# First layer's attention sums: products of rows one and two apart, two rows at a time, with three products in place of four

## The chip, the cores and the metric

The kernel runs on one core of a Trainium2 chip. The metric is device time in microseconds (us) of one launch; lower is better. The engines named below are TensorE (PE, with its weight loads shown as PEld), VectorE (DVE), ScalarE (ACT), GpSimd (POOL) and SyncE (SP, which here issues DMAs).

## The reference

Four layers run one after the other on x of shape (4, 48, 256, 256) in float32, each on the group-normed x and added to it. The change lies in the first layer alone. That layer makes q, k and v by a 1x1 and a depthwise 3x3 convolution and mixes the 48 channels of v by a softmax of the normalised products q k^T over all 65536 pixels.

```python
def _gn(v, G=16, eps=1e-5):
    g = v.reshape(B_, G, C_ // G, H_, W_)
    m = jnp.mean(g, axis=(2, 3, 4), keepdims=True)
    s = jnp.var(g, axis=(2, 3, 4), keepdims=True)
    return ((g - m) / jnp.sqrt(s + eps)).reshape(v.shape)

def _L0_conv_ref(x, qkv_w, dw_w, proj_w, temperature):     # x: (4, 48, 256, 256), f32
    qkv = lax.conv_general_dilated(x, qkv_w, (1, 1), 'VALID', dimension_numbers=DN)
    qkv = lax.conv_general_dilated(qkv, dw_w, (1, 1), ((1, 1), (1, 1)), feature_group_count=3 * c, dimension_numbers=DN)
    q, k, v = jnp.split(qkv, 3, axis=1)
    ...
    q = _l2_normalize(q)
    k = _l2_normalize(k)
    attn = jax.nn.softmax(jnp.einsum('bhcn,bhdn->bhcd', q, k) * temperature, axis=-1)
    out = jnp.einsum('bhcd,bhdn->bhcn', attn, v).reshape(b, c, h, w)
    return lax.conv_general_dilated(out, proj_w, (1, 1), 'VALID', dimension_numbers=DN)
...
x = x + _L0_conv_ref(_gn(x), ...)
x = x + _L1_conv_ref(_gn(x), ...)   # recurrences over rows and columns
x = x + _L2_conv_ref(_gn(x), ...)   # 8x8 patches, products of spectra
x = x + _L3_conv_ref(_gn(x), ...)   # 8x8 patches, mask on spectra, 3x3, gelu
return x
```

## The kernel before

The first stage, `stage_l0_attention`, never builds q and k. All that the attention matrix needs of a picture are sums over pixels of x(p) x(p + shift)^T for the shifts that two 3x3 windows can have between them. With a column of ones added to the 48 channels (C1 = 49), each such sum is a 49x49 product with the pixels as the contracted dimension. The stage collects 29 of them (`l0_terms`): for rows two apart and rows one apart five column shifts each (tile `rows_` in PSUM, 10 x 49 columns), for shifts within a row three (`same`), and terms for the borders (`same` again and `edges`). Afterwards TensorE multiplies them from right and left by the folded weights (`mix_right`, `mix_left`), VectorE multiplies with the taps and adds up, and softmax follows.

**Data.** `x_px` holds the picture as 128 blocks (4 pictures x NBLK = 32) of R = 8 rows. A row is [128 partitions, 6, 49]: 128 pixel pairs, six column positions. Even and odd pixels are two products (`for odd in range(2)`), whose results go to PSUM partitions 0 to 48 and 64 to 112 (ODD = 64), that is to two halves of TensorE's columns. SyncE loads a block (1176 KB) into one of BUF = 4 slots of `l0a_x`, as soon as block n - 3 is used up (semaphore `used`, incremented by the last product of a block).

**Order on TensorE.** Everything is written out by hand. For each row y, `lines` issues one `line` into `same` (147 columns) and then two into `rows_` (245 columns each): the row with the one before it (dy = 1) and with the one two before it (dy = 2), which may lie in the slot before. A line is two matmuls, and each float32 matmul stands in the trace as two instructions. The stationary operand is 49 columns of the earlier row, the moving operand the current row. The first block of a picture is written apart (row 0 has no dy = 1, row 1 no dy = 2), so is the last pass, and the passes between are a hardware loop over four blocks. Between the rows of a picture's first blocks stand the small steps of the picture before: `group_sums` after row (0, 5), `mixing_matrix` after (1, 4), `mix_right` and `mix_left` in block 2, `turn_sum` after row 5 of block 3. In the last pass `turn_scores` and `mix_projection` follow.

**End of a picture.** `borders` puts the column borders into `edges` and increments `sums_done`. Then ScalarE copies the even halves of `same`, `rows_` and `edges` to `r` in SBUF (`r_act`), VectorE the odd halves of `same` and `rows_` (`r_dve`), and TensorE waits for both before the next picture. From `r` VectorE makes the moments of the group norm, and `group_sums` takes them. After the fourth picture the small steps run one after the other with nothing beside them. GpSimd has no work in this stage.

## Time and profile before

| | |
|---|---|
| median of 3 runs | 11938.39 us (11927.18 to 11943.02) |
| profiled execution, its own time | 11946.39 us |
| span of its trace | 11944.6 us |
| TensorE busy over the span | 11372.6 us (95%) |
| VectorE busy | 7033.3 us (59%) |
| ScalarE busy | 5102.7 us (43%) |
| GpSimd busy | 4884.2 us (41%) |
| mean granted clock of TensorE | 0.981 |

The busy times are unions: matmuls overlap each other, so the mean duration of one is longer than what it costs in a row of them. What one costs is therefore read from the distance of starts. The granted clock is a share of full speed; 1.00 is 2.4 GHz and 0.50 is 1.2 GHz.

### The profile page before, as it was taken

Reading aid. Unit: us, or ns where it says so; the run is one execution under the profiler, and the core shown is the slowest. Engines: PE = TensorE matmul, PEld = TensorE weight load, DVE = VectorE, ACT = ScalarE, POOL = GpSimd, SP = SyncE. Lnnn points to the kernel's source line nnn. Section 1 sums busy time; section 2 is a strip of 40 time slices with the busy share of each in tenths; the row PEclk is TensorE's granted clock in tenths of the full one; section 3 lists DMA queues with packets and bytes.
Section 4 is the critical chain, followed back from the end, with each engine's and each line's share of the span. In section 5 each row is a group of like instructions: output and inputs, shape, how many; then the busy total and the mean of one; then the engine's idle time right before and its main releaser. Section 6 shows DMA issues by size and latency. Waiting matters only on the chain. (4 is left out here: it accounts for less than half of the span.)

```text
span 11944.6 us, 374350 instructions
## 1 busy us (share of the span) xinstructions
PE 11372.6 (95%) x155430; PEld 7933.0 (66%) x155430; DVE 7033.3 (59%) x16042; ACT 5102.7 (43%) x10598; POOL 4884.2 (41%) x4142
## 2 busy tenths in 40 slices
PE   8999999989998999899999999999999899889988
PEld 7877544489996777555555555555555577777776
DVE  0000355544444544588888888888888666656665
ACT  0000111134343334355555555555555567767766
POOL 0000122211340025466666666666666444444444
PEclk9999999999998999899999999999999999999999
DMA  4333466597695468866666666666666333333333
GB/s 140 130 133 132 123 160 159 153 159 140 116 163 156 149 178 228 164 85 89 88 88 88 88 88 88 88 88 88 88 89 88 91 104 106 105 96 105 107 103 94
DMA packets 2387653, 1411.49 MB, mean 118 GB/s; under 512 B 1889330, under 2 KB 2260809, under 8 KB 2313245
## 3 DMA queue, kind: packets, MB, share of 16 engines
q1 hardware_dynamic: 2111384, 1290.01, 53.5%
q10 hardware_dynamic: 275072, 105.14, 3.8%
q8 instruction: 797, 13.06, 0.5%
q14 instruction: 400, 3.28, 0.1%
HBM read 646.26 MB, written 449.27 MB: 92 GB/s over the span
## 5 line engine op out<-in xcount | busy, mean ns | idle before, releaser
L1795 PE MATMUL l_m<-l_wa,l_pix 128*128 128x288 f32 x8192 | 2211.2, 413 | 2.7 <-DVE l_wb L1977 2.7
L1795 PEld LDWEIGHTS l_m<-l_wa,l_pix 128*128 128x128 f32 x8192 | 1475.3, 190 | 688.6 <-issue 361.6
L1651 POOL TENSOR_TENSOR l_qkv<-l_qkv,l_copies 128x576 f32<-128x576 f32 x1024 | 1437.1, 1403 | 631.0 <-DVE l_qkv L1988 620.2
L1641 POOL TENSOR_TENSOR l_pix<-l_raw 128x516 f32<-128x516 f32 x1024 | 1217.3, 1189 | 1042.1 <-DVE l_t L2025 1017.2
L1476 PE MATMUL l1h_ps<-l1h_ring,l1h_w 96*96 96x256 f32 x6120 | 1327.3, 379 | 61.5 <-ACT l1h_ring L1418 58.6
L1476 PEld LDWEIGHTS l1h_ps<-l1h_ring,l1h_w 96*96 96x96 f32 x6120 | 998.9, 163 | 389.7 <-issue 58.8
L1509 DVE SCALAR_TENSOR_TENSOR l1h_ring<-l1h_ps,l1h_bias,l1h_columns 96x256 f32<-96x256 f32 x1020 | 670.7, 658 | 677.3 <-PE l1h_ps L1476 671.6
L509 PE MATMUL l0a_rows<-l0a_x 128*49 128x245 f32 x8144 | 1044.2, 371 | 0.0
L870 PE MATMUL l0b_bank<-l0b_x,l0b_w 49*64 49x512 f32 x9216 | 1001.0, 593 | 4.4 <-DVE l0b_w L896 4.4
L1890 ACT ACTIVATE l_ks<-l_f 94x384 f32<-94x384 f32 x1024 | 498.0, 486 | 842.8 <-PE l_f L1810 842.8
L1810 PE MATMUL l_f<-l_qkv,l_a 64*94 64x384 f32 x4096 | 834.7, 483 | 1.6 <-POOL l_qkv L1651 1.5
L870 PEld LDWEIGHTS l0b_bank<-l0b_x,l0b_w 49*64 49x64 f32 x9216 | 437.2, 133 | 565.2 <-issue 565.2
L1801 PE MATMUL l_m<-l_wb,l_left 58*128 58x288 f32 x4096 | 774.2, 455 | 0.0
L1460 POOL TENSOR_TENSOR l1h_columns<-l1h_blocks,l1h_ring 96x2048 f32<-96x2048 f32 x63 | 350.8, 5589 | 1033.1 <-DVE l1h_ring L1509 1033.1
L1901 ACT ACTIVATE l_y<-l_i,l_shift,l_rsd 128x96 f32<-128x96 f32 x2048 | 709.3, 427 | 14.4 <-DVE l_shift L2015 0.6
L1895 ACT ACTIVATE l_sd<-l_mv,l_eps 128x4 f32<-128x4 f32 x512 | 152.2, 297 | 1288.3 <-DVE l_mv L2008 1288.3
L1224 PE MATMUL l1v_ps<-l1v_ring_w,l1v_w 48*48 48x130 f32 x20480 | 632.7, 272 | 46.7 <-ACT l1v_ring_w L1147 41.4
L509 PEld LDWEIGHTS l0a_rows<-l0a_x 128*49 128x49 f32 x8144 | 601.9, 124 | 108.4 <-issue 2.8
L1224 PE MATMUL l1v_ps<-l1v_ring_p,l1v_w 48*48 48x128 f32 x20320 | 616.0, 269 | 7.5 <-issue 7.2
L1224 PEld LDWEIGHTS l1v_ps<-l1v_ring_w,l1v_w 48*48 48x48 f32 x20480 | 586.8, 120 | 50.0 <-issue 50.0
L2568 DVE TENSOR_TENSOR l_gate<-l_turn 128x768 f32<-128x768 f32 x384 | 428.0, 1129 | 301.7 <-ACT l_turn L2478 301.7
L1985 DVE TENSOR_TENSOR l_qkv<-l_m,l_copies 128x288 f32<-128x288 f32 x1024 | 461.9, 451 | 238.4 <-ACT l_copies L1881 223.6
(275 smaller groups left out, 21684.5 us busy)
## 6 DMA issues: line engine op xcount, KB each, us to landing
l0a_x<-x_px_dram SPq DMA_DIRECT2D x128, 1176.0 KB, 5.2
l_edge<-l_turn SPq DMA_DIRECT2D x384, 236.2 KB
l0b_x<-x_in_dram SPq DMA_DIRECT2D x128, 493.8 KB
l_raw<-l_raw SPq DMA_DIRECT2D x128, 483.6 KB, 7.3
l_raw<-x_dram SPq DMA_DIRECT2D x1270, 48.0 KB, 3.7
l_out<-x_dram SPq DMA_DIRECT2D x264, 192.0 KB, 3.6
x_dram<-l0b_out ACTq DMA_DIRECT2D x256, 193.5 KB, 3.1
out_dram<-l_out SPq DMA_DIRECT2D x516, 96.0 KB, 2.0
```

The source lines that it names most:

```text
L509: last = nc.tensor.matmul(o[odd * ODD:odd * ODD + C1, lo:lo + n * C1], x[:, ks, ys, 2 + odd, :], x[:, k, y, e0 + odd:e0 + odd + n, :].rear ...
L870: last = nc.tensor.matmul(bank[2 * n + rt][h * HI:(h + 1) * HI, :], w[part, t, :], rows(part, k, 4 * n + h + t // 3 - rt)[:, :, t % 3:t % ...
L1224: last = nc.tensor.matmul(ps[g][side(c), r, 0:width], w[side(r), t, :], x, start=(t == 0), stop=(t == TAPS - 1), skip_group_check=True)
L1476: last = nc.tensor.matmul(ps[g][0:C2, 0:GI * V], w[:, kernel, s, :], ring[:, g, before % DEEP, :, s:s + V], start=(s == 0), stop=(s == 2))
L1509: nc.vector.scalar_tensor_tensor(out=ring[:, g, x % DEEP, :, 1:V + 1], in0=ps[g][0:C2, 0:GI * V].rearrange("p (i v) -> p i v", i=GI), scal ...
L1641: nc.gpsimd.tensor_tensor(pix[:, n % 2, i, half * HALF:(half + 1) * HALF].rearrange("p (r w) -> p r w", w=PW), in0, in1, op).then_inc(pix_ ...
L1651: nc.gpsimd.tensor_tensor(q, q, copies[:, g % 2, 1:2, :].broadcast_to([128, 2, OUTC]), ALU.add)\
L1795: last = nc.tensor.matmul(bank[i][:, 0:OUTC], pix[:, k, i, first:first + 128], wa[:, b, i, :], start=True, stop=(i in (1, 2)))
L1801: nc.tensor.matmul(bank[i][:, 0:OUTC], left[rows, k, first:first + 128], wb[rows, b, :], start=False, stop=True).then_inc(conv_done, 1)
L1810: last = nc.tensor.matmul(f[0:SLOTS, h, 0:2 * QK].rearrange("p (n o) -> p n o", n=2), a[k, 0:SLOTS], qkv[k, j % 4, 2 * r:2 * r + 2, 0:QK], ...
L1890: nc.scalar.activation(ks[:, r % 2], f[0:SLOTS, :, 0:2 * QK].rearrange("p h (n o) -> p h n o", n=2)[:, :, :, C2:QK], ACT.Copy).then_inc(k_ ...
L1901: last = nc.scalar.activation(y[:, g, m, :], iv[:, m * C2:(m + 1) * C2], ACT.Identity, scale=rsd[:, g, m:m + 1], bias=shift[:, g, m:m + 1])
```

## The change

Rows are taken in pairs. Call the two rows of a pair e (even) and h (odd), the pair before them z and m. Before, rows one apart need <e,h> + <m,e>, and rows two apart <m,h> + <z,e>, where <a,b> is the product of a line with a as stationary and b as moving operand. After, three products are made:

- <m, e + h> into a new PSUM tile `mids`,
- <e - m, h> into the first half of `rows_`,
- <z - m, e> into its second half.

`rows_` first half + `mids` is <e,h> + <m,e>, second half + `mids` is <m,h> + <z,e>. GpSimd makes e + h (`both`, 294 elements per partition) and the two differences (`less`, 98 each) for every pair, one `tensor_tensor` each, and counts them on `paired`, on which TensorE waits once for each pair. Two blocks of `both` and `less` exist (SLOTS = 2): GpSimd starts on block n when n is loaded and block n - 2 is used up. At the end of a picture VectorE adds `mids` to both halves of `r`, in four additions of 49 x 245, before it signals `r_dve`. `edges` now shares the PSUM bank of `zb[0]`. The first pair of a picture has only <e,h>, as before.

```diff
--- before.py
+++ after.py
@@ -423,6 +423,7 @@
     CHUNKS = -(-TERMS // CHUNK)
     EDGE, CORNER = 13, 25
     NCH = 25
+    PAIRS, SLOTS, FORMS = R // 2, 2, 3
     with nc.cleanup_on_exit(), ExitStack() as ctx:
         def sb(name, shape):
             return ctx.enter_context(nc.sbuf_tensor(f"l0a_{name}", shape, F32))
@@ -433,6 +434,8 @@
         def sem(name):
             return nc.alloc_semaphore(f"l0a_{name}")
         x = sb("x", [128, BUF, R, 6, C1])
+        both = sb("both", [128, SLOTS, PAIRS, 6, C1])
+        less = sb("less", [128, SLOTS, PAIRS, 2, 2, C1])
         xc, xk = sb("xc", [128, B, 2, 2, 3, C1]), sb("xk", [4, B, 5, C1])
         first, others = sb("first", [9, O]), sb("others", [9, TERMS, O])
         wt, h = sb("wt", [O, TERMS, O]), sb("h", [O, TERMS, O])
@@ -448,8 +451,9 @@
         n2, rn = sb("n2", [O, 1]), sb("rn", [O, 1])
         sc, e, at = sb("sc", [C, C]), sb("e", [C, C]), sb("at", [C, O])
         mx, sm, rs = sb("mx", [C, 1]), sb("sm", [C, 1]), sb("rs", [C, 1])
-        rows_, same, edges = pb("rows"), pb("same"), pb("edges")
+        rows_, same, mids = pb("rows"), pb("same"), pb("mids")
         zb, qb, small = [pb("z0"), pb("z1")], [pb("q0"), pb("q1")], pb("small")
+        edges = zb[0]
         consts, cleared, w_done, w_out, w_ready = (sem(n) for n in ("consts", "cleared", "w_done", "w_out", "w_ready"))
         taps_in = sem("taps_in")
         loaded = [sem(f"loaded{k}") for k in range(BUF)]
@@ -457,6 +461,8 @@
         chain, spread, rooted, a_done = (sem(n) for n in ("chain", "spread", "rooted", "a_done"))
         z_done, z_out, q_done, h_out = (sem(n) for n in ("z_done", "z_out", "q_done", "h_out"))
         p_turned, turned, exped, mixed = (sem(n) for n in ("p_turned", "turned", "exped", "mixed"))
+        paired, copied = sem("paired"), sem("copied")
+        flat = x[:].rearrange("p k r e c -> p (k r) e c")
         block = ctx.enter_context(nc.Block())
 
         def terms(c):
@@ -501,33 +507,52 @@
             pe.wait_ge(cleared, 2)
             pe.wait_ge(consts, 16 * 9)
 
-            def line(k, y, dy, o, lo, begin, end):
-
-                ks, ys = ((k * R + y - dy) // R) % BUF, (y - dy) % R
-                e0, n = (2, 3) if dy == 0 else (0, 5)
+            def line(k, y, lo, begin, end):
+
                 for odd in range(2):
-                    last = nc.tensor.matmul(o[odd * ODD:odd * ODD + C1, lo:lo + n * C1], x[:, ks, ys, 2 + odd, :],
-                                            x[:, k, y, e0 + odd:e0 + odd + n, :].rearrange("p e c -> p (e c)"),
+                    last = nc.tensor.matmul(same[odd * ODD:odd * ODD + C1, lo:lo + 3 * C1], x[:, k, y, 2 + odd, :],
+                                            x[:, k, y, 2 + odd:5 + odd, :].rearrange("p e c -> p (e c)"),
                                             start=begin, stop=end, skip_group_check=True)
                 return last
+
+            def cross(o, lo, left, right, begin, end):
+
+                for odd in range(2):
+                    last = nc.tensor.matmul(o[odd * ODD:odd * ODD + C1, lo:lo + 5 * C1], left[:, odd, :],
+                                            right[:, odd:odd + 5, :].rearrange("p e c -> p (e c)"),
+                                            start=begin, stop=end, skip_group_check=True)
+                return last
+
+            def pair(turn_of_k, k, y, top, end):
+
+                here, above = k * R + y, (k * R + y - 2) % (BUF * R)
+                if top and y == 1:
+                    return cross(rows_, 0, flat[:, here - 1, 2:4], flat[:, here], True, end)
+                i = y // 2
+                begin = top and y == 3
+                pe.wait_ge(paired, turn_of_k * (BUF * PAIRS * FORMS) + (k * PAIRS + i + 1) * FORMS)
+                cross(mids, 0, flat[:, above, 2:4], both[:, k % SLOTS, i], begin, end)
+                cross(rows_, 0, less[:, k % SLOTS, i, 0], flat[:, here], False, end)
+                return cross(rows_, 5 * C1, less[:, k % SLOTS, i, 1], flat[:, here - 1], begin, end)
 
             def lines(turn_of_k, k, y, top, bottom):
 
                 if y == 0:
                     pe.wait_ge(loaded[k], turn_of_k * 16 + 16)
                 row = y if top else R
-                last = line(k, y, 0, same, 0, row == 0, bottom and y == R - 1)
-                for dy in (1, 2):
-                    if row >= dy:
-                        last = line(k, y, dy, rows_, (dy - 1) * 5 * C1, row == dy, bottom and y == R - 1)
+                line(k, y, 0, row == 0, bottom and y == R - 1)
                 if row == 0:
-                    line(k, y, 0, same, 3 * C1, True, True)
+                    line(k, y, 3 * C1, True, True)
                 if bottom and y == R - 1:
-                    line(k, y, 0, same, 6 * C1, True, True)
+                    line(k, y, 6 * C1, True, True)
+                if y % 2 == 1:
+                    last = pair(turn_of_k, k, y, top, bottom and y == R - 1)
                 if y == R - 1:
                     last.then_inc(used, 1)
 
             def borders(b):
+                if b > 0:
+                    pe.wait_ge(z_out, b * CHUNKS)
                 for col in range(2):
                     for half in range(2):
                         nc.tensor.matmul(edges[0:C1, col * 3 * C1:(col + 1) * 3 * C1], xc[:, b, half, col, 0, :],
@@ -664,8 +689,14 @@
                     dve.wait_ge(z_done, b * CHUNKS)
                 nc.vector.tensor_copy(r[ODD:LAST, 10:19, :].rearrange("p t c -> p (t c)"), same[ODD:LAST, 0:9 * C1])
                 nc.vector.tensor_copy(r[ODD:LAST, 0:10, :].rearrange("p t c -> p (t c)"), rows_[ODD:LAST, 0:10 * C1])\
-                    .then_inc(r_dve, 1)
+                    .then_inc(copied, 1)
+                dve.wait_ge(copied, b + 1)
                 dve.wait_ge(r_act, b + 1)
+                for lanes in (slice(0, C1), slice(ODD, LAST)):
+                    for dy in range(2):
+                        part = r[lanes, 5 * dy:5 * dy + 5, :].rearrange("p t c -> p (t c)")
+                        last = nc.vector.tensor_tensor(part, mids[lanes, 0:5 * C1], part, ALU.add)
+                last.then_inc(r_dve, 1)
                 dve.wait_ge(r_dve, b + 1)
                 nc.vector.tensor_copy(mom[:, 0:1], r[:, 10, C:C1])
                 nc.vector.tensor_tensor_reduce(out=junk[0:LAST, :], in0=r[:, 10, :], in1=diag[0:LAST, :], scale=1.0, scalar=0.0,
@@ -733,6 +764,32 @@
                 dve.wait_ge(mixed, b + 1)
                 nc.vector.tensor_copy(S["mt"][:, b * C:(b + 1) * C], small[0:C, 384:384 + C]).then_inc(chain, 1)
 
+        @block.gpsimd
+        def _(pool):
+
+            def pairs(i, k, first):
+
+                pool.wait_ge(loaded[k], i * 16 + 16)
+                for n in range(PAIRS):
+                    here = k * R + 2 * n + 1
+                    a, m, z = here - 1, (here - 2) % (BUF * R), (here - 3) % (BUF * R)
+                    if first and n == 0:
+                        pool.sem_inc(paired, FORMS)
+                        continue
+                    nc.gpsimd.tensor_tensor(both[:, k % SLOTS, n], flat[:, a], flat[:, here], ALU.add).then_inc(paired, 1)
+                    nc.gpsimd.tensor_tensor(less[:, k % SLOTS, n, 0], flat[:, a, 2:4], flat[:, m, 2:4], ALU.subtract)\
+                        .then_inc(paired, 1)
+                    nc.gpsimd.tensor_tensor(less[:, k % SLOTS, n, 1], flat[:, z, 2:4], flat[:, m, 2:4], ALU.subtract)\
+                        .then_inc(paired, 1)
+            for k in range(BUF):
+                if k >= SLOTS:
+                    pool.wait_ge(used, k - 1)
+                pairs(0, k, k == 0)
+            with pool.Fori(1, B * PASSES) as i:
+                for k in range(BUF):
+                    pool.wait_ge(used, i * BUF + (k - 1))
+                    pairs(i, k, False)
+
 
 def norm_weights(nc, dve, S, b, e, tmp, lb, lb_ready, chain, after):
```

TensorE in the hardware loop, before: the first three rows of a block, where each line in `same` is followed by its two lines in `rows_`.

```order
L509 MATMUL l0a_same<-l0a_x 49x147 [waits l3w_done0]
L509 MATMUL l0a_same<-l0a_x 49x147
L509 MATMUL l0a_rows<-l0a_x 49x245 x4
L509 MATMUL l0a_same<-l0a_x 49x147 x2
L509 MATMUL l0a_rows<-l0a_x 49x245 x4
L509 MATMUL l0a_same<-l0a_x 49x147 x2
L509 MATMUL l0a_rows<-l0a_x 49x245 x4
```

The same place after, two pairs of rows (semaphore l3w_done0 is the number that `loaded1` has here, REGISTER_ALU computes the count to wait for):

```order
L513 MATMUL l0a_same<-l0a_x 49x147 [waits l3w_done0]
L513 MATMUL l0a_same<-l0a_x 49x147 x3
L533 REGISTER_ALU
L521 MATMUL l0a_mids<-l0a_both,l0a_x 49x245 [waits l0a_paired]
L521 MATMUL l0a_mids<-l0a_both,l0a_x 49x245
L521 MATMUL l0a_rows<-l0a_x,l0a_less 49x245 x4
L513 MATMUL l0a_same<-l0a_x 49x147 x4
L533 REGISTER_ALU
L521 MATMUL l0a_mids<-l0a_both,l0a_x 49x245 [waits l0a_paired]
L521 MATMUL l0a_mids<-l0a_both,l0a_x 49x245
L521 MATMUL l0a_rows<-l0a_x,l0a_less 49x245 x4
```

A pair of rows has 4 matmuls of 147 columns in a row and then 6 of 245, where it had 4 and 8 in turns of 2 and 4.

VectorE at the end of the first picture, before:

```order
L665 COPY l0a_r<-l0a_same 49x441 [waits l3w_consts,l0a_sums_done,l3w_cleared,l3w_scaled]
L666 COPY l0a_r<-l0a_rows 49x490
L670 COPY l0a_mom<-l0a_r 113x1 [waits l0a_r_dve,l0a_r_act]
L671 ISA l0a_junk,l0a_mom<-l0a_r,l0a_diag 113x49
```

And after:

```order
L690 COPY l0a_r<-l0a_same 49x441 [waits l3w_consts,l0a_sums_done,l3w_cleared,l3w_scaled]
L691 COPY l0a_r<-l0a_rows 49x490
L698 TENSOR_TENSOR l0a_r<-l0a_mids,l0a_r 49x245 [waits l0a_r_act,l0a_copied]
L698 TENSOR_TENSOR l0a_r<-l0a_mids,l0a_r 49x245 x3
L701 COPY l0a_mom<-l0a_r 113x1 [waits l0a_r_dve]
L702 ISA l0a_junk,l0a_mom<-l0a_r,l0a_diag 113x49
```

Four additions stand between the copies and the moments; TensorE's next picture waits for `r_dve` behind them.

## Rows read from the trace of the kernel before

**Rows 1.** Instructions of line L509: duration ns min/median/max, first and last start.

```profile
L509 PEld LDWEIGHTS l0a_rows<-l0a_x x8144: 122/124/208, 138.1 to 1294.8; 128*49 128x49 f32 x199
L509 PE MATMUL l0a_rows<-l0a_x x8144: 367/370/615, 138.3 to 1295.0; 128*49 128x245 f32 x199
L509 PE MATMUL l0a_same<-l0a_x x4128: 286/288/482, 136.8 to 1295.4; 128*49 128x147 f32 x197
```

**Rows 2.** Busy times by window; the first line names the columns.

```profile
core 0: us, PE busy (x) PEld busy (x) DVE busy (x) ACT busy (x) POOL busy (x), PEclk, DMA share, GB/s
...
300.00:400.00 100.00, 100.00 (x1118) 84.49 (x1116) 0.00 (x0) 0.00 (x0) 0.00 (x0) 1.00 0.38 136
...
136.00:140.00 4.00, 3.15 (x22) 2.70 (x24) 0.00 (x0) 0.00 (x0) 0.00 (x0) 0.50 1.05 435
140.00:144.00 4.00, 4.00 (x32) 2.81 (x30) 0.00 (x0) 0.00 (x0) 0.00 (x0) 0.66 1.03 446
```

**Rows 3.** Timeline inside a picture: start us, duration us, engine, line, instructions.

```profile
603.07 1.03 PE L509 MATMUL l0a_rows<-l0a_x 128*49 128x245 f32 x8
603.69 0.37 PEld L509 LDWEIGHTS l0a_same<-l0a_x 128*49 128x49 f32 x4
603.89 0.46 PE L509 MATMUL l0a_same<-l0a_x 128*49 128x147 f32 x4
...
604.15 1.03 PE L509 MATMUL l0a_rows<-l0a_x 128*49 128x245 f32 x8
604.27 0.33 SPq L479 DMA_DIRECT2D l0a_x<-x_px_dram  x1
...
605.22 1.03 PE L509 MATMUL l0a_rows<-l0a_x 128*49 128x245 f32 x8
```

**Rows 4.** Timeline at the end of the first picture.

```profile
417.37 0.57 ACT L630 ACTIVATE l0a_r<-l0a_edges 49x490 f32<-49x490 f32 x1
...
418.00 0.96 PE L509 MATMUL l0a_same<-l0a_x 128*49 128x147 f32 x12 [1.62 <-ACT l0a_r L630]
...
418.79 0.62 PE L509 MATMUL l0a_rows<-l0a_x 128*49 128x245 f32 x4
...
419.67 1.86 PE L509 MATMUL l0a_rows<-l0a_x 128*49 128x245 f32 x8
...
421.80 1.41 PE L509 MATMUL l0a_rows<-l0a_x 128*49 128x245 f32 x8
...
423.03 0.42 PE L509 MATMUL l0a_same<-l0a_x 128*49 128x147 f32 x4
```

**Rows 5.** Groups by line and shape on VectorE: busy us, mean ns of one.

```profile
L697 DVE TENSOR_TENSOR l0a_h<-l0a_q,l0a_wt 96x480 f32<-96x480 f32 x20 | 13.1, 654 | 65.2 <-PE l0a_q L564 65.2
...
L706 DVE TENSOR_TENSOR l0a_pp<-l0a_s 96x96 f32<-96x96 f32 x4 | 1.0, 254 | 0.1
```

**Rows 6.** Timeline before `turn_sum` of the first picture.

```profile
457.04 0.46 PE L509 MATMUL l0a_same<-l0a_x 128*49 128x147 f32 x4
...
462.15 0.82 DVE L704 TENSOR_REDUCE l0a_s<-l0a_h 96x96 f32<-96x384 f32 x1
...
463.64 0.29 PE L569 MATMUL l0a_small<-k_ident,l0a_pp 96*96 96x96 f32 x1
```

**Rows 7.** Additions of two SBUF tiles on GpSimd: duration ns min/median/max.

```profile
L1651 POOL TENSOR_TENSOR l_qkv<-l_qkv,l_copies x1024: 1389/1403/1417, 5035.5 to 9404.1; 128x576 f32<-128x576 f32 x171
...
L2637 POOL TENSOR_TENSOR l_turn<-l_turn,l_edge x192: 2202/2235/3026, 9468.7 to 11903.1; 128x960 f32<-128x960 f32 x192
...
L1460 POOL TENSOR_TENSOR l1h_columns<-l1h_blocks,l1h_ring x63: 5519/5587/5627, 4325.9 to 4968.2; 96x2048 f32<-96x2048 f32 x63
```

**Rows 8.** GpSimd's timeline, two additions one behind the other.

```profile
7001.00 1.09 POOL L1641 TENSOR_TENSOR l_pix<-l_raw 128x516 f32<-128x516 f32 x1 [2.39 <-DVE l_t L2025]
7002.06 1.41 POOL L1651 TENSOR_TENSOR l_qkv<-l_qkv,l_copies 128x576 f32<-128x576 f32 x1
```

**Rows 9.** The loads of `l0a_x`, from issue to landing.

```profile
DMA to landing us min/median/max: 4.9/5.2/13.0
```

## The prediction

> **What bounds the kernel now.** I read three views, from coarse to fine. The first, the instructions of line L509 [rows 1], gives the length of the stage that changes: its products run from 136.8 to 1295.4 us, 1158.6 us of a span of 11944.6. Nothing outside it is touched, and a stage starts only when the one before it has ended, so what this stage loses or gains goes into the end one to one. The second, busy time by window [rows 2], shows who sets the pace: from 300 to 400 us TensorE is busy 100.00 of 100 us at granted clock 1.00 (2.4 GHz), VectorE, ScalarE and GpSimd 0.00, the DMA share is 0.38. So TensorE bounds the stage, and GpSimd is empty. The third, the timeline within a picture [rows 3], gives the price of one instruction by distances of starts. The 8 instructions into `rows_` take 603.07 to 603.89 = 0.82 us, 102.5 ns each; the 4 into `same` take 603.89 to 604.15 = 0.26 us, 65 ns each. A row is 1.08 us, a block of 8 rows about 8.62 us (5.38 us for five rows of the same timeline would give 8.61). The duration of one (370 and 288 ns in the middle [rows 1]) is no price: they overlap.
>
> 245 columns cost 102.5 ns and 147 cost 65, 0.42 and 0.44 ns per column. The price follows the columns that stream, not the number of instructions.
>
> **The term that the change is made for.** A pair of rows has 8 instructions into `same` and 16 into `rows_` before, 8 and 12 of 245 columns after. Before it is 2.15 us, after 8 x 0.065 + 12 x 0.1025 = 0.52 + 1.23 = 1.75 us. Removed: 4 x 0.1025 = 0.41 us. There are 512 pairs (4 pictures x 128), of which the 4 first ones of a picture stay as they are. 508 x 0.41 = **208.3 us off**. Block time falls to 7.0 us.
>
> Does the new order (8 instructions of `same` in a row instead of 4) keep the price? At a picture's start 12 of them stand in a row [rows 4]: 418.00 to 418.79 is 0.79 us, 66 ns each. Yes.
>
> **GpSimd's side, the unknown.** Each pair needs one addition of 294 elements and two of 98. No GpSimd addition that small is in the trace. From [rows 7], the fastest of 960 (2202 ns) and of 576 (1389 ns) give a slope of 813/384 = 2.12 ns per element and 170 ns fixed. 490 x 2.12 + 3 x 170 = 1.55 us per pair, 6.2 us per block, against TensorE's 1.75 and 7.0. The next one starts a little before the last has ended [rows 8] (1.06 us after one of 1.09), so this is rather high. Other ends: at the pace of the 96 x 2048 additions, (5587 - 170)/2048 = 2.65 ns, a pair is 1.81 us, 0.06 over TensorE's; at the slowest of the 960 ones, (3026 - 170)/960 = 2.98 ns, it is 1.97 us, 0.22 over. I take 1.55: both slow rows are from stages where VectorE works beside GpSimd, and here it is idle. GpSimd may run up to a block ahead, since it starts on block n when TensorE leaves n - 2, so at 1.55 the sums are ready some 5 us before their pair, and the work costs nothing. If that cover went, each 0.1 us per pair would cost 51 us.
>
> **Loads.** GpSimd needs block n one block earlier than TensorE. The load is issued when block n - 3 is used up, lands in 5.2 us [rows 9], and GpSimd wants it 7.0 us later: 1.8 us to spare. The longest, 13.0 us, would be 6 us late; GpSimd's lead of 5 us hides most of that. The DMA share of 0.38 [rows 2] becomes 0.38 x 8.62/7.0 = 0.47. Nothing is added.
>
> **TensorE's 508 added waits.** A wait that is already fulfilled stands in the trace at each block's start, on `loaded`. One lies at about 604.1 us, just ahead of the SyncE issue at 604.27 that the end of the block releases; the rows start 1.08 us before it and 1.07 us after it [rows 3]. Price nil, and I take that, the same kind of wait before the same kind of matmul. Upper end: the start of L569 comes about 0.1 us later than its row's 0.82 us lead to (462.71 + 0.82 for the last row, against 463.64 [rows 6]), though it is another shape as well. 508 x 0.1 would be 51 us.
>
> **End of a picture.** VectorE adds four times 49 x 245 behind its copies. From [rows 5], 654 ns for 480 elements and 254 for 96: 1.04 ns per element, so 254 + 149 x 1.04 = 409 ns each, 1.6 us for four. Before, both waits of TensorE ended with ScalarE's L630 at 417.94 and the next picture began at 418.00 [rows 4]. ScalarE still ends there, and the additions wait for it, so the whole 1.6 us is on the path. It hits three times between pictures and once at the end, where `group_sums` waits for the moments: 4 x 1.6 = **6.4 us lost**. Queued behind the wait is the whole next picture.
>
> **The step `turn_sum`.** It waits for VectorE's sums, which end at 462.15 + 0.82 = 462.97, plus 0.25 for `pp`: 463.22 [rows 5, 6]. Before, six rows stood ahead of it, 457.04 + 6.5 = 463.5, so it came just too late to wait. After, three pairs take 3 x 1.75 = 5.25 us: TensorE is there at 462.3 and waits 0.9 us. Three pictures: **2.8 us lost**. This is the one small step whose cover goes; the others have several us.
>
> **The clock.** After the stop of 1.62 us at 418.00, TensorE ran at full pace, then from 419.67 to about 423 at half pace (1.2 GHz): 2.13 us for a row instead of 1.08 and 1.23 us for 8 instructions instead of 0.82, 1.46 us lost [rows 4]. After the longer emptiness before the stage it ran at 0.50 and then 0.66 [rows 2]: 3.15 x 0.5 + 4 x 0.34 = 2.9 us lost. The stop now becomes 3.2 us, so the loss is between these, 0 to 1.5 us more each. I take half: 3 x 0.75 = **2.2 us**.
>
> **Sum.** 208.3 - 6.4 - 2.8 - 2.2 = 196.9 us less. The profiled execution, 11946.4 us, would be 11749.5. It lies 8.0 us above the median of the runs (11938.4), so the median after is 11741.5 us. The forecast's own range, from its clock and load terms, is 11725 to 11765; with the upper end of the waits 11793.
>
> **Rivals.**
>
> 1. GpSimd sets the pace. For it: at 89% of TensorE's pace it has little room, its price is extrapolated, and both slow rows lie above 1.75. Against it: VectorE is idle beside it. Price: 508 x 0.06 = 30 us at the pace of the 2048 ones (11772), 508 x 0.22 = 112 us at the slowest of the 960 ones (11853).
>
> 2. Weight loads set the pace in the long run of `same`. Loads of four take 0.37 us [rows 3] against 0.26 of streaming. If they paced it, 8 would cost 0.74 instead of 0.52: 508 x 0.22 = 112 us, also 11853. Against it stand the 12 at 66 ns [rows 4]. A sharper form is that no load hides. Then a removed instruction would also give back its load of 124 ns [rows 1], 508 x 4 x 0.124 = 252 us, and the time would be 11490. But 12 loads of 124 ns stand in each row of 1.08 us, less than their sum of 1.49, so they do overlap. The Trainium skill (TensorE: Matmul & The Clock Gate, The mechanism) says that a weight load overlaps with running matmuls only where the row groups differ; all of these use 128 rows, and by that rule 11490 would be the time. The trace does not agree.
>
> 3. **Slower than before:** TensorE catches up with GpSimd, stops, and falls to 1.2 GHz again and again. One such fall costs 1.46 us [rows 4]. With GpSimd at 1.97 us per pair, a block is 7.87 us, and with one fall 9.33 instead of 8.62: 127 x 0.71 = 90 us more than before, 12028. It decides from a pair of (8.62 - 1.46)/4 = 1.79 us on GpSimd, if each block brings a fall. Against it: 1.55 lies under 1.75, and a satisfied wait stops nothing. The Trainium skill has the pattern (same page, A second HAM failure mode: psum-queue depth-cycling): short idle stretches between groups of matmuls make the clock swing. In the trace the four stops between pictures or before them show a fall, and no window without a stop does [rows 2, 4].
>
> 4. The gain does not appear at all, since something else holds the 8.62 us: the loads, or the queue. A load lands in 5.2 us, and 100 us of 100 are busy; little speaks for it. 11938.
>
> **How the numbers follow.** Forecast 0.75 (11725 to 11765, up to 11793 if the waits cost); GpSimd's pace mild, around 11772, 0.10, harsh, around 11853, 0.05; loads pace `same`, 11853, 0.03, unhidden loads 0.01; no gain 0.02; slower by the clock 0.04. The range of 11722 to 11800 holds the first two, 0.85, less some for the edges. A measurement of this kernel can tell 0.2% (24 us) from no change: faster 0.94, same 0.02, slower 0.04.
>
> **What would show it.** Right: products from about 137 to about 1102 us; a pair every 1.75 us in the timeline; TensorE still busy 100 of 100 us within a picture, at clock 1.00; GpSimd busy about 88% there, waiting at each block's start for TensorE (`used`), TensorE never for GpSimd; four additions of about 0.41 us at a picture's end, TensorE's stop there 3.2 us; about 0.9 us before `turn_sum`. Wrong: TensorE waiting for `both` or `less` (rival 1), a low granted clock in mid picture (rival 3), `same` instructions over 80 ns apart (rival 2), or an addition of 98 elements well over 380 ns.

## The result, and the profile after

The changed kernel takes 11747.7 us (median of 4 runs, 11739.89 to 11750.99) against 11939.04 us before: ratio 0.984, 95% interval 0.9823 to 0.9857. The forecast was 11741.5 us in 11722 to 11800. Its sign, its size and its main reason held; GpSimd's price and the clock behind the picture ends were off, and one effect at the stage's end was missing from it.

The instructions of the stage, by line of the changed kernel (duration ns min/median/max, first and last start), answer to [rows 1] and, for GpSimd, to [rows 7]:

```profile
L521 PE MATMUL l0a_rows<-l0a_x,l0a_less x4064: 367/370/615, 140.5 to 1093.6; 128*49 128x245 f32 x194
L521 PE MATMUL l0a_mids<-l0a_both,l0a_x x2032: 369/370/615, 139.7 to 1092.8; 128*49 128x245 f32 x185
...
L779 POOL TENSOR_TENSOR l0a_both<-l0a_x x511: 694/705/719, 126.3 to 1083.7; 128x294 f32<-128x294 f32 x171
...
L780 POOL TENSOR_TENSOR l0a_less<-l0a_x x511: 346/356/407, 126.9 to 1084.4; 128x98 f32<-128x98 f32 x171
...
L698 DVE TENSOR_TENSOR l0a_r<-l0a_mids,l0a_r x16: 394/408/419, 364.6 to 1098.4; 49x245 f32<-49x245 f32 x16
```

The last product starts at 1093.6 us instead of 1295.0. The durations of a single matmul are those of before; there are 6112 of 245 columns instead of 8144.

The timeline inside a picture (start, duration, engine), which answers to [rows 3]:

```profile
501.23 0.75 PE L513 MATMUL l0a_same<-l0a_x 128*49 128x147 f32 x8
501.61 0.33 PEld L521 LDWEIGHTS l0a_mids<-l0a_both,l0a_x 128*49 128x49 f32 x4
501.73 0.66 PE L521 MATMUL l0a_mids<-l0a_both,l0a_x 128*49 128x245 f32 x4
501.77 0.36 POOL L780 TENSOR_TENSOR l0a_less<-l0a_x 128x98 f32<-128x98 f32 x1
...
502.14 1.07 PE L521 MATMUL l0a_rows<-l0a_x,l0a_less 128*49 128x245 f32 x8
502.40 0.71 POOL L779 TENSOR_TENSOR l0a_both<-l0a_x 128x294 f32<-128x294 f32 x1
...
502.97 0.75 PE L513 MATMUL l0a_same<-l0a_x 128*49 128x147 f32 x8
...
503.70 0.70 POOL L779 TENSOR_TENSOR l0a_both<-l0a_x 128x294 f32<-128x294 f32 x1
```

A pair starts every 1.74 us (501.23, 502.97) and GpSimd makes its three forms in 1.30 us (502.40 to 503.70). Who waits is said by the view of waits (us in total, times, longest) for the whole stage:

```profile
POOL l0a_both L779 <- PE l0a_rows L521: 288.4, 124, 12.4
...
PE l0a_same L513 <- issue: 9.6, 3, 3.2
...
PE l0a_small L594 <- DVE l0a_pp L737: 8.6, 4, 6.0
PE l0a_small L566 <- DVE l0a_mom L702: 3.8, 1, 3.8
```

GpSimd waits for TensorE at each block, TensorE never for GpSimd. The three stops of TensorE of 3.2 us at picture ends are there (9.6), and `turn_sum` (L594) has 8.6 - 6.0 = 2.6 us of new waiting in three pictures; the 6.0 is its wait behind the last picture, which was there before.

The windows within a picture and at the stage's end (columns as in [rows 2]):

```profile
200.00:300.00 100.00, 100.00 (x1151) 98.37 (x1149) 0.00 (x0) 0.00 (x0) 74.03 (x171) 1.00 0.47 169
...
1110.00:1115.00 5.00, 5.00 (x29) 4.39 (x28) 0.65 (x1) 1.13 (x2) 0.00 (x0) 0.50 0.00 0
```

TensorE is as full as before, at clock 1.00, with GpSimd 74% busy beside it. The last row is the surprise: in the small steps behind the last picture TensorE stays at 1.2 GHz, where the kernel before came back to 2.4.

**Where the time went.** From the first to the last product of `rows_` (138.3 to 1295.0 before, 137.9 to 1093.6 after): 201.0 us less. Behind it, from the last product of `rows_` to the first matmul of the next stage (called the tail below), 59.5 us instead of 50.1: 9.4 us more. The first product of `rows_` began 0.4 us earlier. So the next stage starts at 1153.1 instead of 1345.1 us, 192.0 earlier, and the medians differ by 191.3. The two profiled executions differ by 206.5; the other 14.5 us lie in later stages that the change doesn't touch (the last layer alone is 8 us shorter in this trace than before, and 20 us longer than here in the trace of c0 below). A single trace is therefore read here by the next stage's start, not by its span.

### The profile page after: what moved, and what is told of

Its sections match the earlier page's. It is cut to its first block and busy times, and to the rows that moved or that the text cites. A ratio compares the mean times of both kernels' runs of the same rounds, so it can differ in the third digit from the quotient of the medians.

```text
span 11738.1 us, 372502 instructions
## 1 busy us (share of the span) xinstructions
PE 11172.0 (95%) x153398; PEld 7853.0 (67%) x153398; DVE 7045.4 (60%) x16058; ACT 5106.1 (44%) x10598; POOL 5558.4 (47%) x5675
## 5 line engine op out<-in xcount | busy, mean ns | idle before, releaser
L872 POOL COPY l0b_x<-l0b_x 49x2322 f32<-49x2322 f32 x128 | 271.4, 2120 | 751.4 <-DMA l0b_x<-x_in_dram 751.4
L1281 PEld LDWEIGHTS l1v_ps<-l1v_ring_p,l1v_w 48*48 48x48 f32 x20320 | 578.7, 120 | 5.6 <-issue 5.6
## 6 DMA issues: line engine op xcount, KB each, us to landing
l_out<-x_dram SPq DMA_DIRECT2D x264, 192.0 KB, 3.6
```

Of the source, the lines that this page charges most:

```text
L1281: last = nc.tensor.matmul(ps[g][side(c), r, 0:width], w[side(r), t, :], x, start=(t == 0), stop=(t == TAPS - 1), skip_group_check=True)
```

## Experiments

### Is it the columns? Four products in the new order, three products without GpSimd

a1 keeps the order of the changed kernel and goes back to four products; GpSimd's work and the additions at a picture's end are left out with it:

```diff
-                pe.wait_ge(paired, turn_of_k * (BUF * PAIRS * FORMS) + (k * PAIRS + i + 1) * FORMS)
-                cross(mids, 0, flat[:, above, 2:4], both[:, k % SLOTS, i], begin, end)
-                cross(rows_, 0, less[:, k % SLOTS, i, 0], flat[:, here], False, end)
-                return cross(rows_, 5 * C1, less[:, k % SLOTS, i, 1], flat[:, here - 1], begin, end)
+                z = (k * R + y - 3) % (BUF * R)
+                cross(rows_, 0, flat[:, above, 2:4], flat[:, here - 1], False, False)
+                cross(rows_, 5 * C1, flat[:, z, 2:4], flat[:, here - 1], begin, False)
+                cross(rows_, 0, flat[:, here - 1, 2:4], flat[:, here], False, end)
+                return cross(rows_, 5 * C1, flat[:, above, 2:4], flat[:, here], False, end)
...
```

> The changed kernel's order, with the four products of before: of each pair of rows the 8 instructions into same in a row, then 16 of 245 columns; no work on GpSimd, no waits on it, no additions at a picture's end. Correct sums. My theory (a row's price follows the columns that stream): a pair costs 0.52 + 1.64 = 2.16 us as before, the time is that of the kernel before, 11939 us within 12. If weight loads paced the long run of same (0.37 us for four), it would be 508 x 0.22 = 112 us more, 12051. If the new order itself gave part of the gain, it would be well under 11915.

Measured: 11946.81 us against 11947.07 of before, ratio 0.9999 (0.999 to 1.0009). The timeline of a1:

```profile
500.64 0.71 PE L513 MATMUL l0a_same<-l0a_x 128*49 128x147 f32 x8
501.15 1.86 PE L521 MATMUL l0a_rows<-l0a_x 128*49 128x245 f32 x16
502.80 0.71 PE L513 MATMUL l0a_same<-l0a_x 128*49 128x147 f32 x8
```

A pair is 2.16 us as before; 8 of `same` take 0.51 us, 64 ns each. The order neither gives nor costs anything, and weight loads don't pace it (rival 2).

a2 takes GpSimd, TensorE's waits for it and the sums and differences out and keeps three products (its attention sums are therefore not the right ones):

```diff
-                pe.wait_ge(paired, turn_of_k * (BUF * PAIRS * FORMS) + (k * PAIRS + i + 1) * FORMS)
-                cross(mids, 0, flat[:, above, 2:4], both[:, k % SLOTS, i], begin, end)
-                cross(rows_, 0, less[:, k % SLOTS, i, 0], flat[:, here], False, end)
-                return cross(rows_, 5 * C1, less[:, k % SLOTS, i, 1], flat[:, here - 1], begin, end)
+                cross(mids, 0, flat[:, above, 2:4], flat[:, here - 1], begin, end)
+                cross(rows_, 0, flat[:, here - 1, 2:4], flat[:, here], False, end)
+                return cross(rows_, 5 * C1, flat[:, above, 2:4], flat[:, here - 1], begin, end)
...
```

> The changed kernel without GpSimd's additions and without TensorE's waits for them: the three products take rows of the picture as they are, so the attention sums leave out the sums and differences of rows. Everything else as changed. My theory: GpSimd's work and the 508 waits cost nothing, the time is that of the changed kernel, 11748 us within 12. If each wait cost 0.1 us it would be 51 us less, 11697.

Measured: ratio 0.984 (0.9824 to 0.9857), the changed kernel's own. (11757.92 us in absolute terms; the kernel before took 11947 beside it.) In its trace the last product starts at 1094.5 and the next stage at 1154.0, where the changed kernel has 1093.6 and 1153.1. So neither GpSimd's 1533 instructions nor TensorE's 508 waits cost anything, and the upper end of 0.1 us for a wait falls.

### What if GpSimd is slower? Twice the work

```diff
...
+                    nc.gpsimd.tensor_tensor(spare[:, k % SLOTS, n], flat[:, a], flat[:, here], ALU.add)
+                    nc.gpsimd.tensor_tensor(rest[:, k % SLOTS, n, 0:2], flat[:, a, 2:4], flat[:, m, 2:4], ALU.subtract)
+                    nc.gpsimd.tensor_tensor(rest[:, k % SLOTS, n, 2:4], flat[:, z, 2:4], flat[:, m, 2:4], ALU.subtract)
                     nc.gpsimd.tensor_tensor(both[:, k % SLOTS, n], flat[:, a], flat[:, here], ALU.add).then_inc(paired, 1)
```

> Each of GpSimd's three operations of a pair done twice, the first time into tiles that nobody reads: 2.59 us for a pair. My theory: 508 x (2.59 - 1.74) = 432 us more than the changed kernel, 12180, slower than before; TensorE stops 0.85 us in each pair, which is shorter than the stop of 1.6 us behind which the clock fell, so the granted clock stays at 1.00. Rival: with stops in each pair the clock falls; at 1.2 GHz a pair takes TensorE 3.5 us, and the time goes towards 11748 + 508 x 1.76 = 12640.

Measured: 12111.16 us, ratio 1.0137 (1.012 to 1.0153), slower than before. One window in mid picture (columns as in [rows 2]) and TensorE's wait in the stage:

```profile
600.00:700.00 100.00, 75.71 (x780) 46.88 (x778) 0.00 (x0) 0.00 (x0) 100.00 (x235) 1.00 0.31 110
```

```profile
PE l0a_mids L523 <- POOL l0a_less L787: 257.8, 420, 0.7
```

GpSimd is full, TensorE idle for a quarter and stopped 420 times for up to 0.7 us, and the granted clock in this window is still 1.00. Inside a picture it fell only twice in the whole stage (0.61 from 508 to 512 us, 0.51 from 840 to 843.5), and both times behind a longer stop, of 4.5 and 4.0 us, ahead of `turn_sum`. So stops of 0.7 us, one in nearly each pair, bring no fall, and rival 3 does not hold at this pace. A milder version with one more addition for each pair (a3, 1.94 us expected on GpSimd against TensorE's 1.74) gave no result, so the pace just above TensorE's, for which the rival was priced, was not measured. The size was off by 69 us (12180 expected): I had added 0.85 us per pair to the changed kernel's time, but GpSimd also works through the picture ends where TensorE stops, so those stops lie within its time. 511 pairs of 2.55 us (6 instructions, at 235 in 100 us) are 1305 us, within 5 us of the distance from 144.0 to 1453.3 us between TensorE's first and last product of this kind.

### Why was GpSimd faster than forecast? VectorE beside it

The line of 2.12 ns per element and 170 ns fixed that I laid through [rows 7] gave 0.79 us for 294 elements and 0.38 for 98. Measured are 0.705 and 0.356: 1.78 ns and 182 ns fixed. b1 lets VectorE add in SBUF while GpSimd works:

```diff
...
             for b in range(B):
                 at0 = b * NCH
+                for n in range(220):
+                    nc.vector.tensor_tensor(spare[:, 0], spare[:, 1], spare[:, 2], ALU.add).then_inc(beside, 1)
+                    dve.wait_ge(beside, b * 220 + n + 1)
                 dve.wait_ge(sums_done, b + 1)
```

> The changed kernel with 220 additions of two SBUF tiles of 128 x 512 on VectorE ahead of each picture's end, each behind the one before, into a tile that nobody reads: VectorE is busy beside GpSimd for some 150 us of each picture. In the changed kernel GpSimd's addition of 294 took 0.705 us and of 98 0.356, below the line of 0.79 and 0.38 that I had laid through the additions of the other stages. Theory: those were stretched by VectorE's work beside them. Then GpSimd's additions become longer here while VectorE works: 0.8 us or more for 294. At 1.37 times (the spread 2202 to 3026 of the 960 ones) a pair is 1.77 us and GpSimd just sets the pace in those stretches, 3 x 0.03 us a block, 5 to 15 us in all. If VectorE does not touch GpSimd, 0.705 stays and so does 11748.

The whole time (12242 us) says nothing: from the second picture on, VectorE's additions began only behind the small steps of the picture before and ran past the picture's end, where TensorE then stood for up to 150 us. That was a flaw of the edit. The first picture is clean. Groups by line and shape on GpSimd (busy us, mean ns of one), first from 200 to 300 us, with VectorE busy beside, then from 360 to 420, without:

```profile
L784 POOL TENSOR_TENSOR l0a_both<-l0a_x 128x294 f32<-128x294 f32 x39 | 44.9, 1152 | 0.0
L785 POOL TENSOR_TENSOR l0a_less<-l0a_x 128x98 f32<-128x98 f32 x38 | 30.6, 804 | 0.0
```

```profile
L784 POOL TENSOR_TENSOR l0a_both<-l0a_x 128x294 f32<-128x294 f32 x34 | 24.0, 706 | 16.0 <-PE l0a_rows L522 14.1 <-DMA l0a_x<-x_px_dram 1.9
...
L785 POOL TENSOR_TENSOR l0a_less<-l0a_x 128x98 f32<-128x98 f32 x34 | 12.1, 356 | 0.0
```

GpSimd's additions become longer by 446 and 448 ns, the same for 294 and for 98 elements. The pace of the pairs then, from the timeline:

```profile
220.10 1.15 POOL L784 TENSOR_TENSOR l0a_both<-l0a_x 128x294 f32<-128x294 f32 x1
...
220.19 0.62 PE L522 MATMUL l0a_mids<-l0a_both,l0a_x 128*49 128x245 f32 x4 [0.69 <-POOL l0a_less L787]
...
222.75 1.15 POOL L784 TENSOR_TENSOR l0a_both<-l0a_x 128x294 f32<-128x294 f32 x1
```

2.65 us for a pair, above the 2.15 us of four products. So GpSimd's work is hidden because VectorE is idle in this stage, and beside a VectorE that adds without a pause the change would lose. The theory (VectorE stretches it) holds, its size did not: I had expected a factor of 1.37, and at the two sizes that were measured it is the same amount for each instruction, about two thirds of a VectorE addition of 512 elements (0.69 us alone, 0.85 in this window). That the additions of [rows 7] were long for this same reason is likely, but no run showed it there.

### The end of a picture and the tail

b2 leaves the four additions out of the changed kernel (`r_dve` is incremented without them, and the attention sums lack the products of `mids`); its edit is shown below. b3 puts four additions of the same size, into a tile that nobody reads, into the kernel before; b0 is the kernel before once more.

```diff
-                for lanes in (slice(0, C1), slice(ODD, LAST)):
-                    for dy in range(2):
-                        part = r[lanes, 5 * dy:5 * dy + 5, :].rearrange("p t c -> p (t c)")
-                        last = nc.vector.tensor_tensor(part, mids[lanes, 0:5 * C1], part, ALU.add)
-                last.then_inc(r_dve, 1)
+                dve.sem_inc(r_dve, 1)
```

> The changed kernel without the four additions at a picture's end: the attention sums leave out the products of mids. Theory: 6.6 us less than the changed kernel, about 11741 where that has 11748 (ratio to before about 0.9835). The stop at a picture's end is 1.6 to 1.7 us again. If the longer stop were what keeps the tail at 1.2 GHz (theory B), 15 us less and a tail of 50 us; under theory A the tail may be 50 or 57.5.

> The kernel before with the changed kernel's four additions of 49 x 245 on VectorE at each picture's end, into a tile that nobody reads, ahead of r_dve. Theory: TensorE's stop goes from 1.6 to 3.2 us at three picture ends and the end of the stage is 1.5 us later: 6 us, and with 0.2 us of clock for each stop 6.6 us more than before (+0.06%). If the longer stop is what keeps the tail at 1.2 GHz (theory B), another 8 us: 15 us more, with a tail of 59.5 us; under theory A the tail may be either 51.5 or 59.5.

> The kernel before, once more, for a second trace of it. In its first trace TensorE came back to 2.4 GHz about 10 us into the small steps behind the last picture, and the stretch from the last product to the next stage's first matmul was 50 us; in the changed kernel and in three products without GpSimd it stayed at 1.2 GHz (59.5 us), and also in four products in pairs (57.4 us), which has no additions. Theory A: whether it comes back there differs from execution to execution or with small shifts in time; then this trace may show either 50 or about 57.5 us. Theory B: it is bound to the changed kernel's longer stop; then 50 us again, with a spread well under 1 us.

Measured: b2 11735.03 us, ratio 0.9818 (0.9801 to 0.9834); b3 1.0002 (0.9993 to 1.0012); b0 1.0001 (0.9992 to 1.0011). A few us are too little for these timings, the traces show them. In the tail TensorE first stops twice, ahead of `group_sums` and ahead of `mixing_matrix`; the column on the clock says in which of the two the granted clock falls to 1.2 GHz, and whether it comes back in the small steps behind them.

| kernel | stop at picture ends | wait of `group_sums` in the tail | clock in the tail | last product to next stage |
|---|---|---|---|---|
| before and b0 | 1.6 | 1.9 | falls in the second stop, comes back | 50.1, 50.0 |
| b3, before + additions | 3.2 | 3.8 | falls in the second stop, comes back | 52.0 |
| b2, changed - additions | 1.7 | 2.0 | falls in the second stop, comes back | 50.1 |
| a1, four products in pairs | 1.7 | 2.0 | falls in the first stop, stays | 57.6 |
| changed and c0 | 3.2 | 3.8 | falls in the first stop, stays | 59.5, 59.5 |
| a2, a4 | 3.2 | 3.8 | falls in the first stop, stays | 59.5, 59.5 |

The additions lengthen a stop by 1.6 us at a picture's end and by 1.9 in the tail, where 1.6 each was forecast. b2's next stage starts 17 us before the changed kernel's (1135.9 against 1153.1 us), not 6.6: the tail's clock and 3 us less of slow stretches (TensorE at 1.2 GHz behind a stop) at the picture ends come on top.

The rest of the changed kernel's 9.4 us in the tail is TensorE's clock in `mix_right` and `mix_left` of the last picture. The timeline of b0:

```profile
1305.10 1.17 PE L564 MATMUL l0a_q<-l0a_a,l0a_z 49*96 49x96 f32 x10
1306.20 1.03 PE L555 MATMUL l0a_z<-l0a_a,l0a_r 113*49 113x96 f32 x10
1307.16 1.08 PE L564 MATMUL l0a_q<-l0a_a,l0a_z 49*96 49x96 f32 x10
```

and of a1, the same instructions on other lines:

```profile
1304.95 1.91 PE L590 MATMUL l0a_q<-l0a_a,l0a_z 49*96 49x96 f32 x10
1306.80 1.83 PE L581 MATMUL l0a_z<-l0a_a,l0a_r 113*49 113x96 f32 x10
1308.56 1.91 PE L590 MATMUL l0a_q<-l0a_a,l0a_z 49*96 49x96 f32 x10
```

At 1.2 GHz such a step takes 1.8 us instead of 1.0. Theory B, that the longer stop keeps the clock down, would fit b2 but falls twice elsewhere: b3 has the long stop and comes back, a1 has the short one and stays. Theory A, that it differs from execution to execution, is not borne out by the two traces that the kernel before and the changed one have each: they agree.

One thing does separate the kernels of the table, and that is when the clock falls. Busy times by window, of the two stops of the kernel before (columns as in [rows 2]; the granted clock is the third number from the end):

```profile
1297.11:1298.97 1.86, 0.00 (x0) 0.00 (x0) 1.49 (x5) 1.81 (x4) 0.00 (x0) 1.00 0.00 0
1299.36:1301.69 2.33, 0.00 (x1) 0.00 (x1) 1.76 (x9) 0.75 (x2) 0.00 (x0) 0.60 0.01 4
```

and of the changed kernel, its first stop and the small steps:

```profile
1095.41:1099.21 3.80, 0.00 (x0) 0.00 (x0) 2.96 (x9) 2.74 (x4) 0.00 (x0) 0.74 0.01 2
...
1103.30:1123.80 20.50, 20.50 (x116) 18.42 (x116) 3.27 (x5) 3.31 (x6) 0.00 (x0) 0.50 0.00 1
```

Where the fall comes in the second stop, TensorE is back at 2.4 GHz about 4 us into the small steps; where it comes in the first, TensorE is busy for 20.5 us without a gap and stays at 1.2 GHz. All nine traces of the table agree with that, and so does c1 below. Why an earlier fall should be kept so much longer stays open, and so does what decides in which stop it comes.

Nor does the length of a stop decide whether the clock falls at a picture's end. b3 has the long stop at all three, and behind the second and the third the clock stays up:

```profile
710.00:722.00 12.00, 8.81 (x95) 6.61 (x95) 4.50 (x18) 2.95 (x5) 0.00 (x0) 1.00 0.28 102
1004.00:1016.00 12.00, 8.81 (x98) 6.81 (x98) 4.72 (x18) 2.95 (x5) 0.00 (x0) 1.00 0.25 97
```

A picture of b3 that begins so takes 288.6 us from its first to its last product, one of the kernel before, behind a shorter stop but with a slow stretch, 290.3: a slow stretch costs 1.7 us. So b3's next stage starts only 2.6 us after that of the kernel before (1347.7 against 1345.1), though its stops are 6.8 us longer in sum.

### A version that is faster than both

c1 takes the added stop ahead of `turn_sum` and part of that at a picture's end away: `turn_sum` moves behind row 7 of block 3, and `mids` is copied to SBUF, so that TensorE goes on behind the copies and the additions run beside it. c2 fills TensorE's two long stops in the tail with matmuls that nobody reads. c3 is both, and c0 the changed kernel again beside them.

```diff
...
+    FILL = (8, 5)
...
-                    pe.wait_ge(r_dve, b)
+                    pe.wait_ge(copied, b)
...
-                            if (k, y) == (3, 5):
+                            if (k, y) == (3, 7):
                                 turn_sum(b - 1)
...
+                nc.scalar.activation(mid[0:C1], mids[0:C1, 0:5 * C1], ACT.Copy)
...
+                nc.vector.tensor_copy(mid[ODD:LAST], mids[ODD:LAST, 0:5 * C1]).then_inc(copied, 1)
...
-                        last = nc.vector.tensor_tensor(part, mids[lanes, 0:5 * C1], part, ALU.add)
+                        last = nc.vector.tensor_tensor(part, mid[lanes], part, ALU.add)
...
+            fill(FILL[0])
             group_sums(B - 1)
+            fill(FILL[1])
             mixing_matrix(B - 1)
```

> The changed kernel once more, beside the three that follow and for a second trace of it. Ratio 0.984 within its interval. The tail (last product to the next stage's first matmul) 59.5 us if TensorE stays at 1.2 GHz in it as in the first trace, about 52 if it comes back as in the kernel before with additions.

> The changed kernel with its two added stops taken away: turn_sum stands behind row 7 of block 3 instead of row 5, and at a picture's end mids is copied to SBUF (ScalarE the even half, VectorE the odd half), TensorE goes on behind these copies, and the four additions run from SBUF beside it. Theory from the traces: 3 x 0.87 us of turn_sum gone, the stop of 3.25 us down to about 2.1, less 0.4 us more ahead of group_sums at the end: 5 to 6 us less than the changed kernel, 0.05%, under what a timing can tell; the trace must show both stops. A rival: the additions then delay the moments until group_sums waits for them, and the gain stays away.

> The changed kernel with matmuls that nobody reads in the two long stops behind the last picture: 8 lines (3.3 us at 2.4 GHz) ahead of group_sums, 5 lines (2.1 us) ahead of mixing_matrix. Theory: TensorE then stays at 2.4 GHz through the small steps; the tail goes from 59.5 us to about 48 (it was 50 where the clock came back on the way), 10 us less than the changed kernel. Rival: the fill is no use, since the clock falls anyway, or the lines run at 1.2 GHz and push the steps back; then 59.5 us or more.

> Both together: 15 us less than the changed kernel, ratio to before about 0.9825 where that has 0.984.

| kernel | median us | ratio to before, interval | last product | tail |
|---|---|---|---|---|
| c0 | 11753.1 | 0.9841 (0.9828 to 0.9855) | 1092.9 | 59.5 |
| c1 | 11734.34 | 0.9827 (0.9814 to 0.9841) | 1081.1 | 59.4 |
| c2 | 11743.0 | 0.9836 (0.9823 to 0.9849) | 1093.0 | 49.8 |
| c3 | 11729.3 | 0.9821 (0.9807 to 0.9834) | 1081.6 | 49.6 |

The intervals of the ratios overlap, but each of the 5 runs of c1 (at most 11737.3 us) and of c3 (at most 11732.6) is faster than each of c0 (at least 11745.0); c2's median lies between. The next stage starts at 1152.4 us in c0 and at 1131.2 in c3, 21 us earlier, and the medians differ by 24. c1 brought twice what I expected of it. Its timeline at the first picture's end:

```profile
363.84 0.96 PE L514 MATMUL l0a_same<-l0a_x 128*49 128x147 f32 x12 [1.88 <-ACT l0a_r L657]
363.89 2.23 DVE L700 TENSOR_TENSOR l0a_r<-l0a_mid,l0a_r 49x245 f32<-49x245 f32 x4 [0.25 <-ACT l0a_r L657]
364.63 0.58 PE L522 MATMUL l0a_rows<-l0a_x 128*49 128x245 f32 x4
365.05 0.67 PE L514 MATMUL l0a_same<-l0a_x 128*49 128x147 f32 x8
365.55 0.58 PE L522 MATMUL l0a_mids<-l0a_both,l0a_x 128*49 128x245 f32 x4
365.96 1.00 PE L522 MATMUL l0a_rows<-l0a_x,l0a_less 128*49 128x245 f32 x8
366.15 0.15 DVE L703 COPY l0a_mom<-l0a_r 113x1 f32<-113x1 f32 x1
...
366.79 0.68 PE L514 MATMUL l0a_same<-l0a_x 128*49 128x147 f32 x8
```

The stop is 1.88 us and behind it the full pace comes at once (12 of `same` in 0.79 us), without the slow stretch. So it is at the third picture's end; at the second one, behind a stop of 1.81 us, TensorE lost 1.6 us to the slow clock (its picture takes 237.8 us, the other two 236.1). In the changed kernel the same place reads:

```profile
366.21 1.24 PE L513 MATMUL l0a_same<-l0a_x 128*49 128x147 f32 x12 [3.25 <-issue]
...
367.98 1.26 PE L513 MATMUL l0a_same<-l0a_x 128*49 128x147 f32 x8
368.96 1.10 PE L521 MATMUL l0a_mids<-l0a_both,l0a_x 128*49 128x245 f32 x4
369.78 1.22 PE L521 MATMUL l0a_rows<-l0a_x,l0a_less 128*49 128x245 f32 x8
370.80 0.70 PE L513 MATMUL l0a_same<-l0a_x 128*49 128x147 f32 x8
```

Over the three ends the changed kernel loses 1.7 + 2.9 + 1.7 = 6.3 us in such slow stretches, c1 1.6. So c1's 11.8 us (1092.9 to 1081.1) are 2.6 of `turn_sum`, 9.6 - 5.5 = 4.1 of the stops and 4.7 of the clock, which makes 11.4. The first two were designed and came out a little above what I had expected; the 4.7 of the clock nobody planned. c3's trace shows it again, but after b3 it can't be put down to the shorter stop, and its cause stays open. The additions there take 2.23 us for four instead of 1.48, now SBUF with SBUF and with GpSimd at work, but TensorE does not wait for them. c2's tail is 49.8 us: both fills hold the clock at 2.4 GHz, though it ends hardly earlier than where the clock comes back by itself (I had said 48), because its `group_sums` waits for the additions: beside b3, which waits for them too and has 52.0 us, it gains 2.2.

## Why the prediction was right, and where not

- **What bounds the stage** (TensorE by streamed columns) and **the main term**: right. Forecast 0.41 us per pair and 208.3 us; measured 2.154 - 1.741 = 0.413, for 508 pairs 209.8 us. a1 and a2 show that it is the fourth product, and not the order, GpSimd or the waits. That a product's price goes by its columns is read from the two sizes (102.5 ns for 245, 65 for 147); no run changed the columns of an instruction alone.
- **Long run of `same`**: right, 64 ns each.
- **GpSimd hidden**: right, by a wider margin than said (1.30 us instead of 1.55). The step that was off is the extrapolation from additions of other stages; GpSimd was busy 74% and not 88%. Its assumption that VectorE's idleness matters was right, and its bounds were too mild: beside a VectorE that adds without a pause the pair is 2.65 us, not 1.97.
- **Waits free**: right, by a2.
- **Additions**: 409 ns each forecast, 408 measured; 6.4 us forecast, 3 x 1.6 + 1.9 = 6.8 measured (stops of 3.25 and 1.62; waits of 3.8 and 1.9).
- **`turn_sum`**: 2.8 forecast, 2.6 measured. It is the kind of cost that only appears because the work ahead of the step got shorter.
- **Clock behind the picture ends**: 2.2 us forecast for the three, 1.3 measured (6.3 us lost instead of 3 x 1.7 = 5.0). The 1.46 us of one stretch, read from [rows 4], was low, since it left out the slow part ahead of 419.67. And the reason given for the term does not hold: that a longer stop costs more clock is refuted by b3, whose stops of 3.2 us cost none at two of three ends. That the term came near is luck. With 209.8 - 4.9 (stops) - 2.6 - 1.3 the products come out at 201.0 us, what the trace has (two shifts of 0.4 us, of the slow stretch at the stage's start and of the order of the last products, cancel).
- **Clock in the tail**: missing. I took only the additions there; TensorE stayed at 1.2 GHz through the last picture's small steps, which costs some 7.5 us. With it the forecast would have been 189.4 us less; the 192.0 measured at the next stage lies above that, since the other terms were off by 2.6 us in all to the other side. So the error of the sum is smaller than that of its largest missing term.
- **Rivals**: 1 did not come, but b1 shows where it would. 2 falls by a1 (64 ns for each of 8 `same` in a row), its sharper form and 4 by the measured time itself. 3 did not come, since TensorE never waits for GpSimd; a4 speaks against it also where TensorE does.

## What to carry to other kernels

Where TensorE streams without a gap, as here, trading one product for sums on an idle engine paid just what the product had cost, and the new order neither added nor took anything. Before counting on GpSimd, look at what VectorE does in the same stretch: here the same additions took 1.6 to 2.3 times as long beside it. And list the small steps that were just covered by the work that you shorten; they become stops, and here moving `turn_sum` two rows down took its stop away.

## What the runs showed of the hardware

- GpSimd, two SBUF operands in float32, 128 partitions, VectorE idle: 356 ns for 98 elements, 705 for 294. With VectorE adding in SBUF beside it: 804 and 1152, 0.45 us more for each instruction at both sizes (b1); VectorE's own additions of 512 went from 0.69 to 0.85 us.
- TensorE stopped up to 0.7 us in nearly each pair, idle a quarter of the time, and kept 2.4 GHz (a4). For longer stops the length did not decide: each of 1.6 us at the picture ends of the kernel before and each of 3.2 us in the changed one brought a fall; of c1's of 1.8 to 1.9 us one did and two did not, of b2's of 1.7 us two did and one did not, and of b3's of 3.2 us one did and two did not.
- TensorE can stay at 1.2 GHz while it is busy without a gap: in a1 and in the changed kernel for the whole of the small steps, 20.5 us at a granted clock of 0.50. In all traces where it stayed, it had fallen in the first of two stops, and where it came back, in the second. Filling both stops (3.8 and 2.3 us) with matmuls avoided the fall in them (c2, c3).
